# One turn of the maxima in eight, in the attention loop, taken as relu of a difference plus the first half

## What is computed

```python
scores = einsum('bhqd,bhkd->bhqk', q, k) * (1 / sqrt(16))
attn = softmax(scores, axis=-1)
x = layernorm(x + einsum('bhqk,bhkd->bhqd', attn, v) @ wo.T + bo)
h = silu(x @ w1.T * s1) * (x @ w2.T * s2)
h = gelu(h @ h1.T * s); h = gelu(h @ h2.T * s)
x = layernorm(x + h @ w3.T * s3)
```

## Time and profile before

| | |
|---|---|
| median of three runs | 442.44 us |
| profiled execution: span | 441.5 us |
| median less span | 0.94 us |
| TensorE matmuls busy | 427.8 us, 97% |
| TensorE weight loads busy | 227.0 us, 51% |
| VectorE busy | 386.5 us, 88% |
| ScalarE busy | 367.7 us, 83% |
| GpSimd busy | 90.3 us, 20% |
| L977, reductions of turn halves | 458 of them |
| TensorE's granted clock | 0.9 or more of full speed in every slice |

### The profile page before, as it was taken

One profiled execution on the slowest core, in us unless ns is written; L12 is line 12 of the kernel. 1 busy time (PEld: TensorE's weight loads), 2 busy tenths in 40 slices (PEclk: granted clock), 3 DMA queues, 4 the chain that ended last, 5 costly groups with the idle time before them and its releaser, 6 DMA issues.

```text
span 441.5 us, 9824 instructions
## 1 busy us (share of the span) xinstructions
PE 427.8 (97%) x3496; PEld 227.0 (51%) x3498; DVE 386.5 (88%) x719; ACT 367.7 (83%) x694; POOL 90.3 (20%) x142
## 2 busy tenths in 40 slices
PE   8999999999999999999999999999899899999995
PEld 4543544444444444444444443544333488877884
DVE  6799999999999999999999999999884577657636
ACT  4487989998998999989899899999899886678762
POOL 9730000100000010000001002373311263046103
PEclk9999999999999999999999999999999999999999
DMA  6567741111130110113011001021021000000101
GB/s 165 176 196 129 270 147 33 44 28 28 48 122 25 45 31 28 27 48 122 25 46 33 26 27 49 14 43 47 15 39 50 13 8 1 1 2 2 48 1 48
DMA packets 17117, 24.88 MB, mean 56 GB/s; under 512 B 5169, under 2 KB 9009, under 8 KB 16689
## 3 DMA queue, kind: packets, MB, share of 16 engines
q1 hardware_dynamic: 16464, 23.68, 19.3%
q10 hardware_dynamic: 608, 0.59, 0.5%
HBM read 15.08 MB, written 7.60 MB: 51 GB/s over the span
## 4 chain that ended last, share of the span: by engine, by line
PE 76%; DVE 10%; ACT 5%; SPq 3%; DMA 2%; issue 2%; POOL 0%; POOLq 0%; DVEq 0%; ACTq 0%
PE ps L1369 24%; PE ps L1291 20%; PE ps L1479 16%; DVE negmax L977 9%; PE ps L1353 8%; ACT arena L664 2%; DMA parts_q<-arena 2%; PE ps L1223 2%; PE ps L1234 1%; PE ps L1423 1%; PE ps L1319 1%; PE ps L1263 1%; SPq L463 1%; SPq L435 1%; ACT v_pad L722 1%
## 5 line engine op out<-in xcount | busy, mean ns | idle before, releaser
L977 DVE TENSOR_REDUCE negmax<-ps 128x1 f32<-128x512 f32 x458 | 275.8, 701 | 1.8 <-PE ps L1291 1.5
L664 ACT ACTIVATE arena<-ps 128x512 f32<-128x512 f32 x360 | 190.0, 606 | 19.3 <-PE ps L1353 14.1
L1353 PE MATMUL ps<-qx,kx 64*128 64x512 f32 x512 | 171.3, 451 | 0.9 <-DMA qx<-mT 0.6
L1291 PE MATMUL ps<-kx,qx 61*128 61x512 f32 x468 | 160.2, 441 | 0.6 <-DMA qx<-parts_q 0.5
L1291 PEld LDWEIGHTS ps<-kx,qx 61*128 61x128 f32 x468 | 75.1, 184 | 88.6 <-DVE negmax L977 79.3
L1369 PE MATMUL ps<-arena,v_pad 128*32 128x256 f32 (+3 forms) x1328 | 104.8, 407 | 2.8 <-ACT arena L664 2.8
L664 ACT ACTIVATE hf<-ps 128x512 f32<-128x512 f32 x152 | 83.2, 604 | 9.4 <-PE ps L1353 8.4
L1353 PEld LDWEIGHTS ps<-qx,kx 64*128 64x128 f32 x512 | 78.9, 184 | 18.6 <-ACT arena L664 11.8
L1479 PE MATMUL ps<-hid,w_high 128*128 128x512 f32 (+1 forms) x296 | 68.3, 388 | 0.8 <-issue 0.4
L1479 PEld LDWEIGHTS ps<-hid,w_high 128*128 128x128 f32 x296 | 54.2, 188 | 12.3 <-issue 0.8
L1369 PEld LDWEIGHTS ps<-arena,v_pad 128*32 128x32 f32 x1328 | 28.5, 108 | 37.1 <-issue 30.7
(11 more groups left out here) (107 smaller groups left out, 317.2 us busy)
## 6 DMA issues: line engine op xcount, KB each, us to landing
qx<-parts_q SPq DMA_DIRECT2D x60, 64.0 KB, 2.1
late_sb<-in_late SPq DMA_DIRECT2D x3, 1280.0 KB, 5.5
kx<-parts_k SPq DMA_DIRECT2D x56, 64.0 KB, 2.2
parts_q<-prt SPq DMA_DIRECT2D x3, 512.0 KB, 6.4
parts_q<-arena SPq DMA_DIRECT2D x3, 512.0 KB, 8.3
xT_sb<-in_xT SPq DMA_DIRECT2D x4, 256.0 KB, 4.2
xT_sb<-arena SPq DMA_DIRECT2D x28, 32.0 KB
prt<-den SPq DMA_DIRECT2D x7, 128.0 KB
```

Of the source, the lines that this page charges most:

```text
L664: nc.scalar.activation(probs(n // HG)[:, heads(n), :], ps[:, PLAN["score", n][0], :], ACT.Exp, scale=SCALE).then_inc(exp_done, 1)
L977: nc.vector.tensor_reduce(negmax[:, t // TURNS % 2, m % 2, h * QT + q:h * QT + q + 1], ps[:, MAX_BANK + m % 4, :], AX.X, ALU.max, negate=T ...
L1291: nc.tensor.matmul(ps[:, half_bank(m), :], qx[at, slot, qc, h, q * P:(q + 1) * P], kx[at, slot, h, part * C:(part + 1) * C], start=True, s ...
L1353: nc.tensor.matmul(ps[:, bank, :], kx[at, slot, h % PAIR, kt * P:(kt + 1) * P], qx[at, slot, qc, h % PAIR, :], start=True, stop=True)\
```

## The change

At 32 turns of units 2 to 15 the second half's matmul is replaced by one with the difference (`kd`), placed first. ScalarE takes its relu behind the three exps of its run. The first half's matmul follows four places later, in the same bank, and VectorE takes both in one pass. The places of the differences are 12 apart (`DIFFS`), each the last place of a run g divisible by four; four such places that lie near a unit's border are left out. The turns' halves are assigned anew to the places (`half_plan`). A fold writes only the first column of negmax; the other is preset by GpSimd.

For this all eight groups need `kd`: the other groups of the first batch are stored with two more DMAs at the start (`store_kd`) and loaded with four (`load_kd(1)`), ahead of the second q block of group 1; the second batch's difference is formed by GpSimd from the projections (`late_apart`), rounded by ScalarE in run 3, stored in the loop, and each group's rows are loaded with four DMAs behind `load_q`. `kd` has two slots. The hardware loops of VectorE, SP and GpSimd are written out.

```diff
+FOLD_GAP = 4
+DIFFS = [p for p in range(AHEAD + RUN - 1, U_ALL * UNIT - 4 * RUN, 4 * RUN)
+         if p >= 2 * UNIT and 2 <= p % UNIT < UNIT - FOLD_GAP]
...
+            def relu(p):
+
+                n = DIFFS.index(p)
+                act.wait_ge(max_scores, p + 1)
+                act.wait_ge(max_taken, taken(DIFFS[n - 2] + FOLD_GAP) if n >= 2 else 2 * WHOLE)
+                nc.scalar.activation(relu_sb(p), ps[:, half_bank(p), :], ACT.Relu).then_inc(relu_done, 1)
...
+                for p in turn_halves(g):
+                    if p in DIFFS:
+                        relu(p)
...
+            def turn_relu(p):
+
+                t, d = HALF[p][0], p - FOLD_GAP
+                dve.wait_ge(max_scores, p + 1)
+                dve.wait_ge(relu_done, DIFFS.index(d) + 1)
+                h, q = head_of(t)
+                nc.vector.tensor_tensor_reduce(relu_sb(d), ps[:, half_bank(p), :], relu_sb(d),
+                                               -1.0, 3.0e38, ALU.add, ALU.min,
+                                               negmax[:, t // TURNS % 2, 0, h * QT + q:h * QT + q + 1])\
+                  .then_inc(max_taken, 1)
...
+                elif m >= 4 and m - 4 in DIFFS:
+
+                    pe.wait_ge(relu_done, DIFFS.index(m - 4) + 1)
...
                 nc.tensor.matmul(ps[:, half_bank(m), :],
-                                       qx[at, slot, qc, h, q * P:(q + 1) * P],
-                                       kx[at, slot, h, part * C:(part + 1) * C], start=True, stop=True)\
+                                 qx[at, slot, qc, h, q * P:(q + 1) * P],
+                                 kd[slot][at, h, :] if part == APART else
+                                 kx[at, slot, h, C * (part == SECOND):C * (part == SECOND) + C], start=True, stop=True)\
...
+            store_kd(0, 1)
+            load_max(0)
             sp.wait_ge(k_out[0], STORE_INC)
             sp.wait_ge(q_out[0], STORE_INC)
             load_k(1, 1, 0, L, rows_in[1][0])
             load_q(1, 1, 0)
+            sp.wait_ge(kd_out[0], STORE_INC)
+            load_kd(1)
             load_q(1, 1, 1)
...
-            with sp.Fori(0, ITERS - 1) as i:
+            for i in range(ITERS - 1):
```

More of the change, by code:

```diff
@@ L89, with half_plan, taken, folded_in @@
 GROUPS_ALL = RUNS + STEPS_ALL - (TAIL - 1)
+UNIT = 2 * TURNS
+FOLD_GAP = 4
+DIFFS = [p for p in range(AHEAD + RUN - 1, U_ALL * UNIT - 4 * RUN, 4 * RUN)
+         if p >= 2 * UNIT and 2 <= p % UNIT < UNIT - FOLD_GAP]
+FIRST, SECOND, APART, FOLDED = range(4)
+def half_plan():
+    plan = {p: (p // 2, p % 2) for p in range(2 * UNIT)}
+    for w in range(2, U_ALL):
+        free, open_turn = [w * TURNS, w * TURNS + 1], [None, None]
+        for p in range(w * UNIT, (w + 1) * UNIT):
+            r = p // 2 % 2
+            if p in plan:
+                continue
+            if p in DIFFS:
+                plan[p], plan[p + FOLD_GAP] = (free[r], APART), (free[r], FOLDED)
+                free[r] += 2
+            elif open_turn[r] is None:
+                plan[p] = free[r], FIRST
+                open_turn[r] = free[r]
+                free[r] += 2
+            else:
+                plan[p] = open_turn[r], SECOND
+                open_turn[r] = None
+    return plan
+HALF = half_plan()
+def taken(p):
+    return p + 1 - sum(1 for d in DIFFS if d <= p)
+def folded_in(w):
+    return [HALF[p][0] for p in DIFFS if p // UNIT == w]
 TURN_AT = {min((2 * TURNS * (w + 1) - 1 - AHEAD) // RUN + 3, RUNS + 1): w for w in range(1, U_ALL)}
@@ L319, in build @@
         kd_set = sem("kd_set")
-        kd_in = sem("kd_in")
+        kd_in = [sem(f"kd_in{slot}") for slot in range(2)]
+        kd_out = [sem(f"kd_out{b}") for b in range(B)]
+        late_apart, late_apart_high, late_apart_low = sem("late_apart"), sem("late_apart_high"), sem("late_apart_low")
+        relu_done = sem("relu_done")
+        none_set = sem("none_set")
         over = sem("over")
@@ L997, in _, with turns_from @@
             dve.wait_ge(max_split, 1)
[L999 to L1006, removed]
+            def turns_from(p0, p1):
+                for p in range(p0, p1):
+                    if HALF[p][1] == FOLDED:
+                        turn_relu(p)
+                    elif HALF[p][1] != APART:
+                        turn_half(p)
+                    if p % UNIT == 0:
+                        larger(p // UNIT - 1)
+            turns_from(2 * WHOLE, INVERT_AT)
             def invert(n):
@@ L1270, in turn_half @@
             def turn_half(m):
-                t, part = m // 2, m % 2
+                t, part = HALF[m]
                 slot, qc, (h, q) = t // (QC * TURNS) % 2, t // TURNS % QC, head_of(t)
@@ L1318, in fold_apart @@
                     pe.wait_ge(over, t - FOLD - len(FOLD_BANKS) + 1)
-                nc.tensor.matmul(ps[:, apart_bank(t), :], rows, kd[at, h, :], start=True, stop=True)\
+                nc.tensor.matmul(ps[:, apart_bank(t), :], rows, kd[0][at, h, :], start=True, stop=True)\
                   .then_inc(max_scores, 1)
```

165 lines of the change are left out of this document (101 added, 64 removed).

## The result

The changed kernel took 450.00 us (median of four runs, 449.50 to 450.73), the kernel before beside it 442.48: 1.0165 times as long [1.0145, 1.0185]. I had forecast 445.4, in a range up to 448.5. The sign was right, the size was not: +7.5 us instead of +3.0.

A forecast was written before the change was run, and what follows sets the result against it. VectorE was taken to bound the loop, with TensorE and ScalarE close behind; +0.8 (runs 9 to 125), +0.4 (125 to 150) and +1.85 (start) make +3.05 us, so 445.4 to 445.5; range 440.0 to 448.5, the forecast's own 444.0 to 447.5.

The forecast's parts named there:

- VectorE sets the pace now; the change frees it: Loop, 80 to 300 us: VectorE bounds it at 1.79 us a run; folds take 18.7 us off, ending that.
- The relu is handed to TensorE by the third score's load: Every fourth run: the relu delays exps that free the third score's bank; 0.24 us a relu, bounds nothing and 0.49.
- Rival (a): Between exps of runs 4k and 4k+1: ScalarE's idle gaps hide the relu; whole kernel 439.2 us; chance 0.17.
- rival (c): Loop: all 18.7 us of VectorE's relief counts, less 1.85 at the start; whole kernel 425.6 us; chance 0.02.
- Freed of VectorE they would take ... together 204.6.: Runs 9 to 125 without VectorE's limit: 116 runs at 1.70 plus 10.9 units at 0.68, 204.6 us against 208.72.
- TensorE is held there anyway; ... 7 of the 26 relus ... So 26 x 0.24 - 7 x 0.19 = 4.9.: Runs 9 to 125: seven relus two runs before a maxima transposition cost about 0.19 less each; relus add 4.9 us.
- Rival (d): Unit borders: relu and unit copy add up, 0.33 a relu; runs 9 to 125 take 211.9, kernel 448.3; chance 0.12.
- Four relus at 0.24: Runs 125 to 150: four relus at 0.24 us each against VectorE relief with little left; +0.4 us net.
- 0.49 (the whole instruction is passed on): Loop: upper bound of a relu's price, its whole ScalarE time paid by TensorE, 0.49 us each; kernel then 453.
- The start, +1.85: Before run 9: four loads of differences ahead of q stores delay unit 1's maxima rows; +1.85 us.
- No cost for the loop's loads and the unrolled loops: Loop: further loads of differences fall where SP waits anyway, and written-out loops cost nothing visible; no added time.
- The time around the span, 0.94: Outside the profiled span: median 442.44 is 0.94 us above the span of 441.5; added to the forecast span of 444.5.

The follow-up runs named there:

- short: Changed kernel with each relu over 16 of 512 columns, order and waits unchanged: 441.47 us, ratio 0.9969 to the kernel before.
- relief: Kernel before, loops written out, VectorE reducing 16 instead of 512 columns at the 32 fold places, no relus or folds: 439.19 us against 442.86.
- relu_only: Kernel before, loops written out, plus 32 SBUF-to-SBUF relus of 128x512 on ScalarE, no folds: 447.72 us, ratio 1.0107.
- run 124: Not an experiment: a group of three turn halves in the kernel's loop, with a fold's relu behind its exps; that relu costs 0.26 us.
- run 126: Not an experiment: the group of three turn halves two after run 124 in the loop, where that run's relu shows its 0.26 us.
- run 144: Not an experiment: a later group of three turn halves in the loop, with a fold's relu behind its exps; that relu costs 0.24 us.
- unrolled: Kernel before with only the VectorE, SP and GpSimd loops written out, no folds or further differences: 442.95 us against 442.96.
- traffic: Changed kernel without any fold, but with all making, stores and loads of the differences: 444.74 us, ratio 1.0049 to the kernel before.
- later: Changed kernel with load_kd(1) moved behind the q stores and unit 1's load_max, too late for the first fold: 458.47 us, ratio 1.0354.

## Why the prediction was right in sign and wrong in size

- **VectorE sets the pace now; the change frees it.** Right. Its idle time went from 0.4 to 11.3 us ("some 10").
- **The relu is handed to TensorE by the third score's load.** Right in mechanism: 0.22 to 0.30 for fifteen of the 25, forecast 0.24, and the short relu takes it away. That the average over all, 5.95 / 25, is 0.24 too is luck, as it is made of four sorts of relu. Rival (a), the hidden relu, and rival (c), the whole relief, are refuted: relief alone brings 3.7 us and not 18.7. But the gap that (a) pointed at is there; it hides half of the relu. Of the two sentences of the Trainium skill ("Perfetto Trace Analysis", Optimizing Scalar/DVE Operations) the one on bubbles fits as far as the relu's length goes, 211.78 against 205.80; breaking it up was not tried. The one on moving work off a saturated VectorE led the wrong way here. The rule of the Trainium skill, "ScalarE: Activation LUTs" (Rules for kernel authors), that relu belongs on VectorE, not on ScalarE, gave the right advice; its reason, the speed per element in bf16, no run here shows. relu_only shows that 32 more relus on ScalarE take 1.0107 times as long.
- **"Freed of VectorE they would take ... together 204.6."** This step failed. relief measures 205.83. With 1.70 a run this is 0.79 a unit, the higher of my two rows, where I took 0.68 because I put part of it down to VectorE. Cost: 1.2 us.
- **"TensorE is held there anyway; ... 7 of the 26 relus ... So 26 x 0.24 - 7 x 0.19 = 4.9."** This step failed as well: 5.95 were measured. By the order of the program only four relus fall two runs before a transposition (12, 44, 76, 108), and they cost 0.27 to 0.30: there is no such discount. Three others are free (40, 72, 104), because the next run waits for the unit's copy, and four pay nearly double, because the copy of the maxima stands in the queue behind them. I had looked at whether TensorE was late there, and not at what comes next on ScalarE. Cost: 1.05 us net. Rival (d) has the number (211.9 for the stretch), but not the place: no relu stands behind the same exps as a unit's copy, and where one is near, the two don't add up.
- **"Four relus at 0.24" in runs 125 to 150.** Failed: they cost 48.05 - 46.08 = 1.97 against relief. One belongs to a fifth relu, that of run 124, which acts in run 126 (0.26); that of run 144 costs 0.24; the other three, of runs 132, 136 and 140, together 1.47 or 0.49 each, the whole instruction. In the short kernel the next instruction starts 0.06 behind all three, so no gap was left there. The first and the last of them share the gap between two runs' exps with the rounding of a weight slice, as in the rows below from the timeline of the changed kernel; a run ahead of the second (294.82) one stands too, at 292.87. The upper bound of "0.49 (the whole instruction is passed on)" was the price there. That it is the roundings that had used up the gaps fits, but no kernel without them was run. Relief gave back 0.39.

```profile
286.52 0.59 ACT L738 ACTIVATE hf<-ps 128x512 f32<-128x512 f32 x1
287.00 0.61 ACT L753 ACTIVATE arena<-ps 128x512 f32<-128x512 f32 x1
287.48 0.64 ACT L800 ACTIVATE w_high<-late_sb 128x512 fp32r<-128x512 f32 x1
288.00 1.59 ACT L738 ACTIVATE hf<-ps 128x512 f32<-128x512 f32 x3
```

- **The start, +1.85.** Right: +1.98, and run 9 at 59.53 (forecast 59.4). The detail was not: the last store of q is issued 3.05 later but takes 0.9 less to land.
- **No cost for the loop's loads and the unrolled loops.** Right: 208.72 and 208.71.
- **The time around the span, 0.94.** Wrong: it is 1.7. I took the median of three runs less the span of another execution.

Of the 4.5 us that were missing (7.5 less 3.0), 2.3 lie in runs 9 to 125, 1.2 in runs 125 to 150, 0.1 at the start, and 1.2 in comparing one execution with a median; the end of the kernel took 0.3 less. What that 0.3 is (the end takes 128.4 in relief, short and relu_only too, and 128.7 in unrolled and traffic), and why the start of run 9 differs by up to 0.7 us between kernels that do the same up to there (56.82 to 57.55), was not tested.

## What to carry to other kernels

An engine's busy share doesn't say what an added instruction costs. Follow the buffer that its end frees: if that buffer is already reused without slack, the instruction is passed on, less the gap in which its engine would have waited. Here the gap hid half of it, and hardly anything where what stands behind it in the queue (the copy of the maxima, a rounding) was ready to start. The gap can be read from a kernel in which the added instruction is kept but made very short. Before work is moved off the bounding engine, measure the next limit with a kernel that only drops the work; here it was 3.7 us away, and the relus that were to buy it cost 7.9 (5.95 and 1.97).

## What the hardware showed unexpectedly

- After TensorE had stood still for 9.3 us (in later), its granted clock was 0.50 of full speed, the level of 1.2 GHz, in the windows from 54 to 62 us, 0.55 from 62 to 64, and 1.00 from 64 on, although it had been busy without a gap since 58.
- A relu of 128x512 held ScalarE for 0.48 us from PSUM (in the changed kernel) and 0.52 from SBUF to SBUF (in relu_only), start to start, though their recorded durations, 0.62 and 0.64, hardly differ.
- The last store of q took 7.4 us to land behind four more loads in the queue, and 8.3 without them; its issue took 1.32 us instead of 0.92.
